# Variance products on the rounded squares and their remainder, placed one transpose later

## The chip, the cores and the metric

The kernel runs on one core of one Trainium2 chip. The metric is the device time of one execution in microseconds (us). The profile is one execution, recorded by the hardware profiler.

## The reference

The input is 8 sequences of 256 tokens with 128 channels. One attention layer of 16 heads comes first, then a stack of six layers, each with local attention (16 heads of 64, window 32) and a gated feed-forward part. The change lies in the feed-forward part's layer norm:

```python
def ffn_layer(x, g, bln, W1, b1, W2, b2):
    mu = x.mean(-1, keepdims=True)
    var = ((x - mu) ** 2).mean(-1, keepdims=True)
    xn = (x - mu) / jnp.sqrt(var + 1e-05) * g + bln
    hg = xn @ W1 + b1
    a, gate = jnp.split(hg, 2, -1)
    return a * jax.nn.gelu(gate, approximate=False) @ W2 + b2
for i in range(DEPTH):
    x = attn_layer(shift_tokens(x), Wqkv[i], q_scale[i], k_scale[i], Wo[i]) + x
    x = ffn_layer(shift_tokens(x), ln_g[i], ln_b[i], W1[i], b1[i], W2[i], b2[i]) + x
```

## The kernel before

After the first attention (some 280 us) the six layers are worked off as 6 x 8 = 48 units, one sequence in one layer each. A unit's activations lie as 128 channels (partitions) x 256 tokens, in two tiles `t` of 128 tokens. Every engine runs the same software pipeline: `step` works on four neighbouring units at once, `after`, `u` (projection, rope, transposes), `before` (softmax and values) and `last` (output projection, layer norm and feed-forward). The order inside `step` is written out by hand for each engine, and each engine works its own list strictly in that order. Semaphores (`signal`) tie the lists together: an engine that reaches a wait stops there, and so does all that stands behind it in its list.

The functions that matter, with the lines of the profile:

- TensorE, `proj(u, t, j)` (L1910, L1915, L1919): one of 16 projections of a unit into one of two PSUM banks. A bank is free again when the copy or rope that reads what lay in it is done: proj(u, 1, 1) waits for `un` on ScalarE, proj(u, 1, 2) and proj(u, 1, 3) wait for the two ropes of tile 1 on DVE.
- TensorE, `transpose_qk` (L1934): four transposes into the bank TP; waits for `normalise` on GpSimd and for the copy `qT` or `kT` on ScalarE that empties TP. `transpose_p` (L1966): eight transposes of the softmax.
- TensorE, `feed_mean` (L1999, L2000): x minus its mean, by a product with a centering matrix, into the bank FB. `feed_var` (L2009): the mean of the squares of each token, two products whose stationary operand is a tile of squares (128 x 128) and whose moving operand is one column of 1/128. `feed_turn` (L2018) transposes the reciprocal root back over all partitions. `feed_w1` (L2035 to L2037) is the first feed-forward product, on operands split into a rounded part and a remainder.
- ScalarE, `copy_center` (L1747, xc), `square_x` (L1754, xq), `copy_u` (L1660, un), `square` (L1650, sq), `copy_qkT` (L1672 qT, L1676 kT).
- DVE, `feed_3` (L1553): variance plus epsilon to `vtok`. Behind it in DVE's list stand `rope(u, 1, 0, 0)` and `rope(u, 1, 0, 1)` (L1486).
- GpSimd, `turn` (L1346, two halves), `normalise` (L1408), `feed_w1_lo` (L1399, in some of the units), `feed_rstd` (L1382, rtok = vtok to the power -0.5), `feed_lo` (L1389, xg_lo).

`F32R` is the format of the rounded operands, four bytes each; `F32` is full precision. The lists around the change, as they were before:

```python
# TensorE                      # GpSimd                 # DVE
transpose_qk(u, 0, 0, 0)       normalise(u, 0, 0)       soft_shift(before, 1)
feed_var(last)                 turn(u, 0, 1, 0)         feed_3(last)
proj(u, 1, 1)                  turn(u, 0, 1, 1)         rope(u, 1, 0, 0)
transpose_qk(u, 0, 0, 1)       feed_w1_lo(last)         rope(u, 1, 0, 1)
transpose_p(before, 0)         feed_rstd(last)          sums(u, 1, 0)
feed_turn(last)                normalise(u, 0, 1)       feed_norm(last)
```

Of the kernel before, what the change touches and what calls it, by code (L numbers as in the profile page):

```python
# [31 lines left out]
P = 128  # L32
# [57 lines left out]
def build(nc, x, w_heads, bq_heads, bk_heads, w_v, b_v_rows, w_proj, b_proj_rows, wqk, q_scale_rows, k_scale_rows, wvt, wo,  # L90
          feed_cols, w1, w2, rope, ident, win_mask, win_pick, causal, positions, slope_heads, one_row, weights, out):
    with ExitStack() as ctx:
        def sb(name, shape, dt=F32):
            return ctx.enter_context(nc.sbuf_tensor(name, shape, dt))

        def signal(name, per=1, start=0):
            return Signal(ctx.enter_context(nc.semaphore(name)), per, start)
# [89 lines left out]
        x2l_d = signal("x2l_d")  # L187
        xc_a = signal("xc_a")
        xq_a = signal("xq_a")
        var_p = signal("var_p")  # L190
        vr_d = signal("vr_d")
        rr_g = signal("rr_g")
# [1010 lines left out]
        xc = sb("xc", [P, T])  # L1203
        xe = sb("xe", [P, 2, T])
        xq = sb("xq", [P, T])
        vtok = sb("vtok", [P, TT])
        rtok = sb("rtok", [P, TT])
        xg = sb("xg", [P, T])
# [7 lines left out]
        def index(u):  # L1216

            return u[0] * 2 + u[1]
# [15 lines left out]
        def live(u):  # L1234

            n = index(u)
            return not isinstance(n, int) or 0 <= n < UNITS
# [7 lines left out]
        with nc.Block() as block:  # L1245
# [80 lines left out]
            def _(pool):  # L1326
# [50 lines left out]
                def feed_rstd(u):  # L1377
# [3 lines left out]
                    pool.wait_ge(vr_d.sem, vr_d.at(n))  # L1381
                    G.tensor_tensor(rtok[:, :], vtok[:, :], minus_half[:, :], ALU.pow).then_inc(rr_g.sem, 1)  # L1382

                def feed_lo(u):
                    if not live(u):
                        return
                    n = index(u)
                    pool.wait_ge(xgh_a.sem, xgh_a.at(n))
                    G.tensor_tensor(xg_lo[:, :], xg[:, :], xg_hi[:, :], ALU.subtract).then_inc(xgl_g.sem, 1)  # L1389
# [20 lines left out]
                def step(m, s):  # L1410
                    after, u, before, last = ((m, s + k) for k in (1, 0, -1, -2))
                    clamp(before, 1)
                    norms(before, 1, 0)
                    norms(before, 1, 1)
                    norms(before, 1, 2)
                    norms(before, 1, 3)
                    norms(before, 1, 4)
                    norms(before, 1, 5)
                    norms(before, 1, 6)
                    norms(before, 1, 7)  # L1420
                    normalise(before, 1, 0)
                    turn(before, 1, 1, 0)
                    turn(before, 1, 1, 1)
                    normalise(before, 1, 1)
                    turn(u, 0, 0, 0)
                    shift_lo(after)
                    turn(u, 0, 0, 1)
                    clamp(u, 0)
                    norms(u, 0, 0)
                    norms(u, 0, 1)  # L1430
                    norms(u, 0, 2)
                    norms(u, 0, 3)
                    norms(u, 0, 4)
                    norms(u, 0, 5)
                    norms(u, 0, 6)
                    norms(u, 0, 7)
                    normalise(u, 0, 0)
                    turn(u, 0, 1, 0)
                    turn(u, 0, 1, 1)
                    feed_w1_lo(last)  # L1440
                    feed_rstd(last)
                    normalise(u, 0, 1)
                    turn(u, 1, 0, 0)
                    turn(u, 1, 0, 1)
                    feed_lo(last)
# [4 lines left out]
            def _(dve):  # L1450
# [4 lines left out]
                dve.wait_ge(tables_ready.sem, 1)  # L1455
                dve.sem_inc(fin_d.sem, 1)
                dve.wait_ge(ident_in.sem, 16)
                V.tensor_scalar(center[:, :], ident_s[:, :], 1.0 / C, None, ALU.subtract).then_inc(center_d.sem, 1)

                def add_shifted(u, add):  # L1460
# [87 lines left out]
                def feed_3(u):  # L1548
                    if not live(u):
                        return  # L1550
                    n = index(u)
                    dve.wait_ge(var_p.sem, var_p.at(n))
                    V.tensor_scalar(vtok[:, :], ps[:, FB, T:T + TT], LN_EPS, None, ALU.add).then_inc(vr_d.sem, 1)  # L1553

                def feed_norm(u):
                    if not live(u):
# [79 lines left out]
            def _(act):  # L1636
# [112 lines left out]
                def square_x(u):  # L1749
                    if not live(u):  # L1750
                        return
                    n = index(u)
                    act.wait_ge(mean_p.sem, mean_p.at(n))
                    S.activation(xq[:, :], ps[:, FB, 0:T], ACT.Square).then_inc(xq_a.sem, 1)  # L1754

                def feed_scale(u):
# [103 lines left out]
            def _(pe):  # L1860
# [141 lines left out]
                def feed_var(u):  # L2002
                    if not live(u):
                        return
                    n = index(u)
                    pe.wait_ge(xc_a.sem, xc_a.at(n))
                    pe.wait_ge(xq_a.sem, xq_a.at(n))
                    for t in range(TT):
                        last = M.matmul(ps[:, FB, T + t:T + t + 1], xq[:, t * P:(t + 1) * P], mean_w[:, 0:1], start=True, stop=True)  # L2009
                    last.then_inc(var_p.sem, 1)  # L2010

                def feed_turn(u):
# [46 lines left out]
                def step(m, s):  # L2059
# [19 lines left out]
                    transpose_qk(u, 0, 0, 0)  # L2079
                    if index(last) == UNITS - 2:  # L2080
                        keep_warm(10, PJ)
                    feed_var(last)
                    if index(last) == UNITS - 1:
                        finish_turn(2)
                        finish_turn(3)
                    proj(u, 1, 1)
                    transpose_qk(u, 0, 0, 1)
                    transpose_p(before, 0)
                    feed_turn(last)
                    if index(last) == UNITS - 1:  # L2090
# [137 lines left out]
```

## Time and profile before

| | |
|---|---|
| median of 3 runs | 1670.52 us (1668.34 to 1673.65) |
| the profiled execution | 1671.68 us, span 1669.9 us |
| granted clock of TensorE, mean | 0.990 |
| TensorE matmul busy | 1621.9 us (97%) |
| TensorE weight load busy | 1412.5 us (85%) |
| DVE busy | 1478.7 us (89%) |
| ScalarE busy | 1327.9 us (80%) |
| GpSimd busy | 1333.4 us (80%) |

The span runs from the first to the last instruction; the time of an execution is a little longer. PE stands for TensorE's matmuls, PEld for its weight loads, which overlap them; ACT is ScalarE, POOL is GpSimd. In the timeline, bracketed text at a row's end is the idle time of that engine before it and what ended it. Matmul ends are modelled, so starts are the safer figures.

### The profile page before, as it was taken

The numbers are of one execution on the slowest core, as the hardware profiler recorded it, in microseconds if no ns is written. First come the engines' busy times: TensorE is split into PE (matmuls) and PEld (weight loads), VectorE is DVE, ScalarE is ACT, GpSimd is POOL, SyncE is SP. The second block draws the span as 40 slices with busy tenths as digits, with TensorE's granted clock in tenths as the row PEclk, the third lists the DMA queues.
The fourth block names the chain that finished last, engine by engine and source line by source line (L and its number), as shares of the span: only waits on it lengthen the run. The fifth ranks groups of instructions, "written<-read, shape, count | busy, mean of one in ns | idle before, by whom it ended". The sixth has DMA issues, their size and how long they took to land.

```text
span 1669.9 us, 70686 instructions
## 1 busy us (share of the span) xinstructions
PE 1621.9 (97%) x29222; PEld 1412.5 (85%) x29222; DVE 1478.7 (89%) x2314; ACT 1327.9 (80%) x2801; POOL 1333.4 (80%) x1810
## 2 busy tenths in 40 slices
PE   7999969999999999999999999999999999999997
PEld 5777647898989889898988889898898988889886
DVE  6887748999999999899999999999999999999984
ACT  6888836888878788887888788788888888888874
POOL 7777568888888888888888788888888888888870
PEclk9999979999999999999999999999999999999999
DMA  3588507566865656857566766658566567656654
GB/s 126 172 299 313 213 11 160 129 151 138 228 161 129 150 122 151 235 135 162 121 150 180 184 149 140 145 120 251 129 157 144 132 152 214 156 126 147 141 130 113
DMA packets 101407, 265.78 MB, mean 159 GB/s; under 512 B 26720, under 2 KB 34912, under 8 KB 101088
## 3 DMA queue, kind: packets, MB, share of 16 engines
q1 hardware_dynamic: 101088, 261.26, 61.9%
q8 instruction: 232, 3.80, 1.0%
q14 instruction: 87, 0.71, 0.1%
HBM read 45.15 MB, written 27.26 MB: 43 GB/s over the span
## 4 chain that ended last, share of the span: by engine, by line
PE 80%; POOL 2%; SPq 1%; issue 1%; DVE 1%; ACT 1%; DMA 0%; POOLq 0%; ACTq 0%; DVEq 0%
PE ps L1910 18%; PE ps L1919 14%; PE ps L1978 10%; PE ps L1934 10%; PE ps L1956 8%; PE ps L1966 5%; PE ps L2048 4%; PE ps L2035 2%; PE ps L2037 2%; PE ps L2036 2%; PE ps L1948 2%; SPq L1262 1%; PE ps L2009 1%; PE ps L1915 1%; PE ps L1989 1%
## 5 line engine op out<-in xcount | busy, mean ns | idle before, releaser
L1346 POOL TENSOR_TENSOR rot<-rot 128x512 f32<-128x512 f32 x380 | 491.4, 1309 | 43.5 <-DVE rot L1486 43.4
L1486 DVE TENSOR_TENSOR rot<-ps,rope_l 128x1024 f32<-128x1024 f32 x380 | 462.6, 1218 | 21.1 <-ACT sq L1650 13.0
L1408 POOL TENSOR_TENSOR rot<-rot,rnorm 128x1024 f32<-128x1024 f32 x190 | 361.9, 1905 | 17.7 <-POOL rnorm L1374 0.4
L1660 ACT ACTIVATE un<-ps 128x512 f32<-128x512 f32 x384 | 229.4, 597 | 105.4 <-PE ps L1910 42.3
L1910 PE MATMUL ps<-w_t,xs_hi 128*128 128x512 f32 x880 | 298.0, 419 | 3.7 <-DVE rot L1486 1.7
L1919 PE MATMUL ps<-w_t,xs_hi 128*128 128x256 f32 x1284 | 262.9, 297 | 14.2 <-PEq L375 11.0
L1650 ACT ACTIVATE sq<-ps 128x512 f32<-128x512 f32 x380 | 227.5, 599 | 48.8 <-PE ps L1910 27.4
L1472 DVE TENSOR_REDUCE ssum<-sq 128x16 f32<-128x1024 f32 x190 | 229.8, 1210 | 14.0 <-ACT sq L1650 14.0
L1934 PE MATMUL ps<-ident_s,rot 128*128 128x128 f32 x1536 | 233.9, 275 | 2.6 <-POOL rot L1408 1.1
L1919 PEld LDWEIGHTS ps<-w_t,xs_hi 128*128 128x128 f32 x1284 | 196.4, 190 | 24.6 <-issue 20.4
L1934 PEld LDWEIGHTS ps<-ident_s,rot 128*128 128x128 f32 x1536 | 179.3, 140 | 36.9 <-issue 17.3
L1978 PE MATMUL ps<-vk,pT 128*32 128x128 f32 (+1 forms) x6624 | 189.6, 267 | 0.6 <-ACT pT L1693 0.6
L1919 PE MATMUL ps<-w_t,xs_lo 128*128 128x256 f32 x642 | 180.6, 281 | 0.0
L1978 PEld LDWEIGHTS ps<-vk,pT 128*32 128x32 f32 x6624 | 163.9, 110 | 16.6 <-issue 15.6
L1910 PEld LDWEIGHTS ps<-w_t,xs_hi 128*128 128x128 f32 x880 | 139.1, 190 | 33.6 <-ACT un L1660 7.6
L1910 PE MATMUL ps<-w_t,xs_lo 128*128 128x512 f32 x389 | 154.5, 397 | 0.0
L1956 PEld LDWEIGHTS ps<-kT,qT 64*32 64x32 f32 x12288 | 146.8, 106 | 7.3 <-issue 1.2
L1956 PE MATMUL ps<-kT,qT 64*32 64x64 f32 x12288 | 149.7, 226 | 0.5 <-issue 0.5
L1919 PEld LDWEIGHTS ps<-w_t,xs_lo 128*128 128x128 f32 x642 | 121.4, 189 | 0.0
L1530 DVE TENSOR_TENSOR prob<-ps,linv 128x1024 f32<-128x1024 f32 x96 | 117.6, 1225 | 3.1
L1497 DVE TENSOR_REDUCE smax<-ps 128x16 f32<-128x1024 f32 x96 | 116.4, 1213 | 3.9 <-PE ps L1956 3.9
L1514 DVE TENSOR_REDUCE lsum<-ps 128x16 f32<-128x1024 f32 x96 | 116.6, 1215 | 2.7 <-ACT ps L1684 2.7
(158 smaller groups left out, 3572.0 us busy)
## 6 DMA issues: line engine op xcount, KB each, us to landing
vk<-un SPq DMA_DIRECT2D x1440, 128.0 KB
w_t<-weights_dram SPq DMA_DIRECT2D x48, 512.0 KB, 6.9
weights_dram<-rot SPq DMA_DIRECT2D x12, 1024.0 KB, 5.1
weights_dram<-sq SPq DMA_DIRECT2D x24, 512.0 KB, 3.5
raw<-wqk_dram SPq DMA_DIRECT2D x24, 256.0 KB, 4.2
wvt_s<-wvt_dram SPq DMA_DIRECT2D x12, 256.0 KB, 5.2
wo_s<-wo_dram SPq DMA_DIRECT2D x12, 256.0 KB, 6.4
w_s<-w_dram SPq DMA_DIRECT2D x6, 341.0 KB, 3.5
```

Source lines behind the costliest of these rows:

```text
L1346: last = G.tensor_tensor(cos[:, :, s, :], cos[:, :, s, :], sin[:, :, 1 - s, :], ALU.add)
L1408: G.tensor_tensor(v, v, rnorm[:, t, kind * H:(kind + 1) * H, None].broadcast_to([P, H, D]), ALU.mult).then_inc(nrm_g.sem, 1)
L1472: V.tensor_reduce(ssum[:, t, kind * H:(kind + 1) * H], sq[:, kind, :].rearrange("p (h e) -> p h e", h=H), AX_X, ALU.add).then_inc(ss_d.sem, 1)
L1486: V.tensor_tensor(dst, src[:, None, :, :].broadcast_to([P, 2, H // 2, D]), tab[:, :, None, :].broadcast_to([P, 2, H // 2, D]), ALU.mult).t ...
L1530: V.tensor_tensor(pairs, tile_scores(t).rearrange("p (hp a) k -> p hp a k", hp=2), inv, ALU.mult).then_inc(pn_d.sem, 1)
L1650: S.activation(sq[:, kind, half * 512:(half + 1) * 512], ps[:, PJ + PJ_BANK[t][2 * kind + half], :], ACT.Square).then_inc(sq_a.sem, 1)
L1660: S.activation(un[:, (u[1] % 2) * TT + t, j // 2, (j % 2) * HALF:(j % 2 + 1) * HALF], ps[:, PJ + PJ_BANK[t][QK_BANKS + j], :], ACT.Copy).t ...
L1910: last = M.matmul(bank, v, w_t[:, j, w, :], start=i == 0, stop=i == 2)
L1919: last = M.matmul(bank[:, cols], v, w_t[:, j, w, cols], start=i == 0, stop=i == 2)
L1934: last = M.transpose(ps[:, TP, a * P:(a + 1) * P], rot[:, kind, 0, c * P:(c + 1) * P], ident_s[:, :])
L1956: last = M.matmul(out_s, qT[rows, par, a, 32 * w:32 * w + 32], kT[rows, a, 32 * w:32 * w + 64], start=False, stop=a == PAIRS - 1)
L1978: last = M.matmul(ps[32 * k:32 * k + 32, SO[t], cols], pT[:, a, 32 * k:32 * k + 32], vk[:, 4 * t + k, a, cols], start=a == 0, stop=a == PA ...
```

## The change

The squares are written twice by ScalarE from the same PSUM bank, once rounded to F32R (`xq_hi`), once in full (`xq`). GpSimd subtracts the one from the other into `xq_lo`, F32R as well. Each variance product becomes two accumulating ones, with `xq_hi` and `xq_lo` as stationary operands, and the moving operand has two columns of 1/128 (`mean_r`), so that each result takes two columns of the bank, of which `feed_3` reads the first. `feed_var` waits for GpSimd's subtract in place of ScalarE's square, and stands two places later in TensorE's list. `square_lo` stands between the two halves of `turn(u, 0, 1)` on GpSimd.

```diff
+        xql_g = signal("xql_g")
...
+        xq_hi = sb("xq_hi", [P, T], F32R)
+        xq_lo = sb("xq_lo", [P, T], F32R)
+        mean_r = sb("mean_r", [P, 2], F32R)
...
+                def square_lo(u):
+                    if not live(u):
+                        return
+                    n = index(u)
+                    pool.wait_ge(xq_a.sem, xq_a.at(n))
+                    G.tensor_tensor(xq_lo[:, :], xq[:, :], xq_hi[:, :], ALU.subtract).then_inc(xql_g.sem, 1)
...
                     turn(u, 0, 1, 0)
+                    square_lo(last)
                     turn(u, 0, 1, 1)
...
+                V.tensor_copy(mean_r[:, :], mean_w[:, 0:2])
...
-                    V.tensor_scalar(vtok[:, :], ps[:, FB, T:T + TT], LN_EPS, None, ALU.add).then_inc(vr_d.sem, 1)
+                    V.tensor_scalar(vtok[:, :], ps[:, FB, T:T + 2 * TT].rearrange("p (t k) -> p t k", k=2)[:, :, 0], LN_EPS, None, ALU.add).then_inc(vr_d.sem, 1)
...
+                    S.activation(xq_hi[:, :], ps[:, FB, 0:T], ACT.Square)
                     S.activation(xq[:, :], ps[:, FB, 0:T], ACT.Square).then_inc(xq_a.sem, 1)
...
-                    pe.wait_ge(xq_a.sem, xq_a.at(n))
+                    pe.wait_ge(xql_g.sem, xql_g.at(n))
                     for t in range(TT):
-                        last = M.matmul(ps[:, FB, T + t:T + t + 1], xq[:, t * P:(t + 1) * P], mean_w[:, 0:1], start=True, stop=True)
+                        for i, v in enumerate((xq_hi, xq_lo)):
+                            last = M.matmul(ps[:, FB, T + 2 * t:T + 2 * t + 2], v[:, t * P:(t + 1) * P], mean_r[:, :], start=i == 0, stop=i == 1)
...
-                    feed_var(last)
...
                     proj(u, 1, 1)
                     transpose_qk(u, 0, 0, 1)
+                    feed_var(last)
                     transpose_p(before, 0)
                     feed_turn(last)
```

TensorE's list in a unit from the middle of the run, from the first transposes of the unit to feed_turn. The names in brackets are the semaphores waited for: `un_a1` is copy_u of tile 1, `qkT_a` the copy out of TP, `nrm_g` normalise, `pn_d` the softmax, `rr_g` rtok. Before:

```order
L1934 MATMUL ps<-ident_s,rot 128x128 [waits qkT_a,nrm_g]
L1934 MATMUL ps<-ident_s,rot 128x128 x3
L2009 MATMUL ps<-mean_w,xq 128x1 [waits xq_a,xc_a]
L2009 MATMUL ps<-mean_w,xq 128x1
L1910 MATMUL ps<-w_t,xs_hi 128x512 [waits un_a1]
L1910 MATMUL ps<-w_t,xs_hi 128x512
L1910 MATMUL ps<-w_t,xs_lo 128x512
L1934 MATMUL ps<-ident_s,rot 128x128 [waits qkT_a,nrm_g]
L1934 MATMUL ps<-ident_s,rot 128x128 x3
L1966 MATMUL ps<-ident_s,prob 128x128 [waits pn_d]
L1966 MATMUL ps<-ident_s,prob 128x128 x7
L2018 MATMUL ps<-ident_s,rtok 128x128 [waits rr_g]
```

With the change (the kernel's lines have other numbers there):

```order
L1924 MATMUL ps<-w_t,xs_hi 128x512 [waits un_a1]
L1924 MATMUL ps<-w_t,xs_hi 128x512
L1924 MATMUL ps<-w_t,xs_lo 128x512
L1948 MATMUL ps<-ident_s,rot 128x128 [waits qkT_a,nrm_g]
L1948 MATMUL ps<-ident_s,rot 128x128 x3
L2024 MATMUL ps<-mean_r,xq_hi 128x2 [waits xql_g,xc_a]
L2024 MATMUL ps<-mean_r,xq_lo 128x2
L2024 MATMUL ps<-mean_r,xq_hi 128x2
L2024 MATMUL ps<-mean_r,xq_lo 128x2
L1980 MATMUL ps<-ident_s,prob 128x128 [waits pn_d]
L1980 MATMUL ps<-ident_s,prob 128x128 x7
L2033 MATMUL ps<-ident_s,rtok 128x128 [waits rr_g]
```

The variance products left the place in front of proj(u, 1, 1) and stand behind the next four transposes, four single products in place of two, and they wait for `xql_g`.

GpSimd's list in the same place, in a unit with a piece of W1. Before:

```order
L1346 TENSOR_TENSOR rot<-rot 128x16x32 [waits rope_d]
L1346 TENSOR_TENSOR rot<-rot 128x16x32
L1399 TENSOR_TENSOR w_lo<-w_s,w_hi 128x226 [waits w1_p,w1h_a]
L1382 TENSOR_TENSOR rtok<-vtok,minus_half 128x2 [waits vr_d]
L1408 TENSOR_TENSOR rot<-rot,rnorm 128x1024 [waits newton_g,turn_g]
```

With the change:

```order
L1350 TENSOR_TENSOR rot<-rot 128x16x32 [waits rope_d]
L1393 TENSOR_TENSOR xq_lo<-xq,xq_hi 128x256 [waits xq_a]
L1350 TENSOR_TENSOR rot<-rot 128x16x32
L1410 TENSOR_TENSOR w_lo<-w_s,w_hi 128x226 [waits w1_p,w1h_a]
L1386 TENSOR_TENSOR rtok<-vtok,minus_half 128x2 [waits vr_d]
L1419 TENSOR_TENSOR rot<-rot,rnorm 128x1024 [waits newton_g,turn_g]
```

The subtract came between the two halves of the turn, with a wait of its own for ScalarE's squares (`xq_a`).

## Rows read from the trace of the kernel before

**Rows 1.** Windows view, one unit: us, busy PE, PEld, DVE, ACT, POOL; clock; DMA.

```profile
1256.05:1285.22 29.17, 29.17 (x570) 26.26 (x569) 27.37 (x32) 23.85 (x45) 24.28 (x33) 1.00 0.63 142
```

**Rows 2.** The chain that ended last: shares, then pieces (start us, us, what).

```profile
PE 80%; POOL 2%; SPq 1%; issue 1%; DVE 1%; ACT 1%; DMA 0%; POOLq 0%; ACTq 0%; DVEq 0%
...
1256.56 0.81 PE ps L1910 x3
...
1258.89 1.40 PE ps L1910 x6
```

**Rows 3.** Groups by line, and two rows of the timeline (start us, us).

```profile
L2009 PEld LDWEIGHTS ps<-mean_w,xq 128*128 128x128 f32 x192 | 25.2, 192 | 0.6 <-ACT xc L1747 0.6
L1999 PEld LDWEIGHTS ps<-x_hi,center 128*128 128x128 f32 x48 | 9.0, 188 | 3.4 <-DVE x_lo L1546 1.2 <-issue 0.4
...
1253.93 0.28 PE L1999 MATMUL ps<-x_hi,center 128*128 128x256 f32 x1
...
1254.05 0.28 PE L2000 MATMUL ps<-x_lo,center 128*128 128x256 f32 x1
```

**Rows 4.** The timeline, weight loads of TensorE: start us, us, engine, line, tiles.

```profile
1255.94 0.53 PEld L2009 LDWEIGHTS ps<-mean_w,xq 128*128 128x128 f32 x4
...
1256.39 0.30 PEld L1910 LDWEIGHTS ps<-w_t,xs_hi 128*128 128x128 f32 x2
...
1257.01 0.54 PEld L1934 LDWEIGHTS ps<-ident_s,rot 128*128 128x128 f32 x4
...
1257.53 0.91 PEld L1966 LDWEIGHTS ps<-ident_s,prob 128*128 128x128 f32 x8
...
1258.40 0.25 PEld L2018 LDWEIGHTS ps<-ident_s,rtok 128*128 128x128 f32 x2
...
1258.62 0.30 PEld L1910 LDWEIGHTS ps<-w_t,xs_hi 128*128 128x128 f32 x2
...
1259.31 0.30 PEld L1910 LDWEIGHTS ps<-w_t,xs_hi 128*128 128x128 f32 x2 [0.16 <-DVE rot L1486]
...
1259.89 0.59 PEld L1934 LDWEIGHTS ps<-ident_s,rot 128*128 128x128 f32 x4
...
1262.92 0.19 PEld L2035 LDWEIGHTS ps<-xg_hi,w_hi 128*128 128x128 f32 x1
```

**Rows 5.** The timeline, ScalarE.

```profile
1254.62 0.38 ACT L1747 ACTIVATE xc<-ps 128x256 f32<-128x256 f32 x1
...
1254.89 0.39 ACT L1754 ACTIVATE xq<-ps 128x256 f32<-128x256 f32 x1
...
1255.15 0.62 ACT L1660 ACTIVATE un<-ps 128x512 f32<-128x512 f32 x1
...
1255.81 0.60 ACT L1650 ACTIVATE sq<-ps 128x512 f32<-128x512 f32 x1
...
1256.31 0.59 ACT L1672 ACTIVATE qT<-ps 128x512 f32<-128x512 f32 x1
```

**Rows 6.** The timeline, DVE.

```profile
1256.59 0.16 DVE L1553 TENSOR_SCALAR vtok<-ps 128x2 f32<-128x2 f32 x1 [0.88 <-PE ps L2009]
1256.67 2.58 DVE L1486 TENSOR_TENSOR rot<-ps,rope_l 128x1024 f32<-128x1024 f32 x2
...
1262.09 2.43 DVE L1486 TENSOR_TENSOR rot<-ps,rope_l 128x1024 f32<-128x1024 f32 x2
```

**Rows 7.** The timeline, GpSimd.

```profile
1253.00 2.73 POOL L1346 TENSOR_TENSOR rot<-rot 128x512 f32<-128x512 f32 x2
...
1256.83 0.72 POOL L1382 TENSOR_TENSOR rtok<-vtok,minus_half 128x2 f32<-128x2 f32 x1 [1.11 <-DVE vtok L1553]
...
1257.52 1.90 POOL L1408 TENSOR_TENSOR rot<-rot,rnorm 128x1024 f32<-128x1024 f32 x1
...
1259.38 2.53 POOL L1346 TENSOR_TENSOR rot<-rot 128x512 f32<-128x512 f32 x2
...
1261.93 0.73 POOL L1389 TENSOR_TENSOR xg_lo<-xg,xg_hi 128x256 fp32r<-128x256 f32 x1
```

## Prediction

> **What bounds the kernel now.** I read the busy table of one steady unit first, then the chain that ended last, then the timeline of the stretch that the change touches, engine by engine.
>
> One unit of the pipeline (one sequence in one layer) takes 29.17 us [rows 1], from one variance product to the next, and 48 units make up most of the span. In it TensorE is busy all 29.17 us at a granted clock of 1.00, DVE 27.37, ScalarE 23.85, GpSimd 24.28. So TensorE has no slack, DVE has 1.80 us a unit, the other two about 5. The chain of the whole run agrees: 80% of it lies on TensorE [rows 2]. Hence two rules for costing: whatever makes TensorE wait, or adds passes to it, lengthens every unit; what another engine does longer costs nothing until its result comes later than TensorE asks for it. The averages don't say where that is, so the rest is a walk through the unit that starts at 1256.05.
>
> **The products themselves: 0 us.** The 96 variance products appear as 192 loads and 192 matmuls of one column [rows 3]: a full-precision product is already two passes here, so a unit has four. The products on tiles of the rounded format appear once each (center, x48 for 48 units), so four of them are four passes again. A load of 128 rounded columns takes 188 ns, of full ones 192 ns [rows 3]. The four loads hold the load queue for 1256.39 - 1255.94 = 0.45 us [rows 4]; products of the rounded format follow each other at 1254.05 - 1253.93 = 0.12 us [rows 3], so 0.48. I take 0.45 before and after.
>
> The Trainium skill, "TensorE: Matmul & The Clock Gate", section on weight-path perf modes, says that fast weight load is on for 128 weights of a type other than FP32 and measured about twice the speed. Taken for the rounded format, it would make the four loads about half as long, and an estimate by it is 0.22 us less for a unit. The 188 ns against 192 of rows 3 don't show it.
>
> **ScalarE squares twice: +0.27 us a unit, not hidden.** ScalarE's small operations overlap; they start 1254.89 - 1254.62 = 0.27 apart though each lasts 0.38 [rows 5]. So un, sq and qT behind the square start 0.27 later. un and sq run without a gap before them, and qT (the copy that frees the transpose bank) ends at 1256.90; the load of the next transposes starts at 1257.01, 0.11 later [rows 4, 5]. That load is therefore already held by ScalarE about as much as by TensorE's own order. With qT at 1256.58 + 0.59 = 1257.17 it starts at **1257.28 (+0.27)**. Taking the variance block away from in front of proj(1,1) brings nothing: TensorE is ready 0.45 earlier and then waits for this copy (proj(1,1) itself needs un, ready at 1256.04).
>
> **GpSimd's subtract: 0 us.** It waits for xq, which now ends at 1254.89 + 0.27 + 0.39 = 1255.55. A result reaches the next engine about 0.08 later, as vtok's end at 1256.75 does rtok's start at 1256.83 [rows 6, 7]. So it starts at 1255.63 and takes what xg_lo takes, 0.73 [rows 7]: ready at 1256.36. The products ask for it later than 1257.7. The second half of turn(0,1), half of the pair of 2.73, moves to 1256.36 to 1257.7. Behind it GpSimd stood idle 1.11 before rtok [rows 7] (less in units with a piece of w1_lo there), and rtok will wait longer still (below), so the 0.73 lies in that idle time. Without that cover it would cost 0.73 a unit.
>
> **The products move behind transpose_qk(0,0,1): this is the cost.** That transpose holds the load queue 1257.53 - 1257.01 = 0.52 [rows 4], so the variance loads start at 1257.28 + 0.52 = 1257.80 instead of 1255.94 (+1.86), and the transposes of transpose_p at 1258.25 instead of 1257.53 (+0.72). From the first variance load to vtok are 1256.59 - 1255.94 = 0.65 [rows 4, 6], so vtok starts at 1258.45. Two things hang on it.
>
> - DVE. Ahead of vtok in the queue DVE is idle, [0.88 <-PE ps L2009]; behind it stand the two ropes of tile 1 [rows 6], and they free the banks of proj(1,2) and proj(1,3). Now they start at 1258.45 + 0.08 = 1258.53. Without a wait between them two take 2.43 (the pair at 1262.09) [rows 6], so the first frees its bank at 1259.75, the second at 1260.96. Today the pair ends at 1256.67 + 2.58 = 1259.25 and the load of proj(1,3) starts at 1259.31 with [0.16 <-DVE rot L1486] [rows 4]: the bank is already the thing waited for. So it now starts at 1260.96 + 0.06 = 1261.02, **+1.71**. Proj(1,2) is held to 1259.81 (+1.19); its own 0.69 would let proj(1,3) start at 1260.50, so the second rope decides.
> - GpSimd. rtok starts at 1258.61 + 0.08 = 1258.69 and ends at 1259.41; feed_turn's load, 1258.40 today [rows 4], comes at 1259.50 (+1.10), which lies under the +1.19. normalise(0,1) starts 0.69 after rtok's start [rows 7] and ends at 1261.28; transpose_qk(0,1,0) asks for it at 1259.89 + 1.71 = 1261.60, so it doesn't wait. The next pair of turns starts 1.86 behind it, xg_lo 2.55 after that, at 1263.79, and ends at 1264.52; the load of the first W1 product asks at 1262.92 + 1.71 = 1264.63 [rows 4, 7]. Also just hidden.
>
> After that every engine is 1.7 to 1.8 behind, and none has anything to catch up with, TensorE having had no slack. The unit becomes 29.17 + 1.71 = 30.88 us.
>
> **Sum.** 46 units in which projections run beside it: 46 x 1.71 = 78.7. In the last two units none do; there the chain itself gets longer by 0.27 + 0.73 + 0.08 = 1.1, so 2.2. The copy of mean_w is one instruction. Total 81 us. The profiled execution took 1671.68 (span 1669.9): 1752.7. The median of the runs is 1.2 lower: **1752**, 4.9% slower. Below: if only one of the two late results counted, 1.10 a unit. Above: matmuls of the rounded format behind full ones start slowly, three take 0.81 there and 1.40 / 2 = 0.70 otherwise [rows 2]; the moved block makes one more such change, +0.11, and GpSimd's two hits with 0.1 to spare may miss by up to 0.3: 2.1 a unit. Forecast's own range 1.5 to 1.95 a unit: 1740 to 1761.
>
> **The rivals.**
> - *feed_turn alone decides* (0.12). The ropes' lateness is absorbed by DVE's 1.80 idle and TensorE waits just for rtok: 46 x 1.10 + 2.2 = 53, so 1723. For it: DVE's slack is about as large as its delay. Against: the slack lies before vtok, not behind it, and a wait on the rope is in the trace already.
> - *Not slower: TensorE alone decides, and loads of the rounded tiles pass in half the time* (0.06). The place is the block of four loads: 0.45 / 2 = 0.22 less, 48 times, 10.8 us: 1660; with full-length loads 1670.5, no change. It decides if a load takes under 0.1 us and the load of proj(1,3) isn't later than now. For it: averages leave every other engine room. Against: rows 3, and 0.88 of idle DVE in front of vtok can't pay for 1.86. The load rule of the Trainium skill's page named above points to this case; by it, with the waits as I walk them, the unit would grow by 1.49 instead of 1.71.
> - *More than forecast* (0.12): the slow start and GpSimd's misses come on top, 2.1 a unit: 1670.5 + 46 x 2.1 + 2.2 = 1769. The same price would follow if the edit didn't do what it says and a rounded product with two columns ran in two passes (0.45 more a unit); the x48 of center speaks against that.
>
> **How the numbers follow.** Forecast 0.70, the rivals 0.12, 0.06, 0.12. The range takes in most of both outer cases that are slower: 1720 to 1772. A change under 0.3% (5 us) can't be told from none with this kernel. Faster by more 0.03, within 0.03 (both from the second rival), slower 0.94.
>
> **What the changed profile would show.** Variance loads still x192, near 190 ns. DVE's idle time before vtok grows from 0.9 to about 2.7 us a unit, and TensorE's loads show waits for DVE's rot in front of proj(1,2) and proj(1,3), and a wait for ScalarE's qT in front of transpose_qk(0,0,1). GpSimd's waits for xq_a and vtok stay, without TensorE waiting for xq_lo. The unit is 30.9 us. I am wrong if proj(1,3) isn't waiting on rot, or if vtok starts less than 1.5 us later beside the transposes than it did.

## The result, and the profile after

The changed kernel takes 1736.72 us (median of 4 runs, 1734.71 to 1737.97), the kernel before 1671.64 in the same count of runs: ratio 1.0359, 95% interval 1.0329 to 1.0388. By the two medians it is 65 us slower; the ratio given is not the quotient of these two medians (1.0389, just above the interval) and stands for 60 us. 1752 was forecast, with a range of 1720 to 1772. The page of the changed kernel begins:

```profile
span 1732.9 us, 70783 instructions
...
PE 1665.7 (96%) x29222; PEld 1407.6 (81%) x29222; DVE 1473.0 (85%) x2315; ACT 1349.5 (78%) x2849; POOL 1365.6 (79%) x1858
```

The instruction counts of TensorE are those of before (29222), while the span grew by 63 us. Its busy time grew by 44 us of these for the same instructions, since the ends of its matmuls are modelled and hide part of a wait; the loads show the waits better. The windows view of one unit, in the columns of [rows 1]:

```profile
1297.69:1328.23 30.54, 30.18 (x572) 26.14 (x569) 27.29 (x32) 24.31 (x46) 24.96 (x35) 1.00 0.63 143
```

A unit now takes 30.5 us. Taken over all units, the distance from one vtok to the next has a median of 30.48 us against 29.16 before: **+1.32 a unit**, where 1.71 was forecast. The work of DVE and GpSimd in it is what it was plus the subtract. The loads of the variance products, in groups by line (they answer to [rows 3]):

```profile
L2024 PEld LDWEIGHTS ps<-mean_r,xq_lo 128*128 128x128 f32 x96 | 18.7, 195 | 0.0
L2024 PEld LDWEIGHTS ps<-mean_r,xq_hi 128*128 128x128 f32 x96 | 18.6, 194 | 1.1 <-issue 1.0
```

192 in all, at 194 to 195 ns: four passes a unit as before, and no shorter loads. The list of waits (who waited for whom, us in total, times, longest):

```profile
DVE vtok L1566 <- PE ps L2024: 114.1, 48, 2.8
POOL xq_lo L1393 <- ACT xq L1768: 76.7, 48, 16.8
...
PEld ps L1924 <- DVE rot L1499: 35.5, 83, 1.4
...
PEld ps L2033 <- POOL rtok L1386: 17.9, 48, 1.3
```

DVE's wait for the variance was 38.5 us before and is 114.1; TensorE's loads wait for ropes and for rtok. Now the same stretch as in [rows 4 to 7], from the timeline of the changed kernel (start us, us, engine, line). Its xc starts 40.14 later than in the unit of before, so 40.14 taken off brings both on one clock.

```profile
1294.76 0.38 ACT L1760 ACTIVATE xc<-ps 128x256 f32<-128x256 f32 x1
...
1295.29 0.41 ACT L1768 ACTIVATE xq<-ps 128x256 f32<-128x256 f32 x1
...
1295.77 0.73 POOL L1393 TENSOR_TENSOR xq_lo<-xq,xq_hi 128x256 fp32r<-128x256 f32 x1 [1.03 <-ACT xq L1768]
...
1296.50 0.65 ACT L1685 ACTIVATE qT<-ps 128x512 f32<-128x512 f32 x1
...
1297.27 0.42 PEld L1948 LDWEIGHTS ps<-ident_s,rot 128*128 128x128 f32 x4 [0.51 <-issue]
...
1297.66 0.19 PEld L2024 LDWEIGHTS ps<-mean_r,xq_hi 128*128 128x128 f32 x1
...
1298.13 0.86 PEld L1980 LDWEIGHTS ps<-ident_s,prob 128*128 128x128 f32 x8
...
1298.31 0.16 DVE L1566 TENSOR_SCALAR vtok<-ps 128x2 f32<-128x2 f32 x1 [2.33 <-PE ps L2024]
1298.39 2.36 DVE L1499 TENSOR_TENSOR rot<-ps,rope_l 128x1024 f32<-128x1024 f32 x2
1298.55 0.72 POOL L1386 TENSOR_TENSOR rtok<-vtok,minus_half 128x2 f32<-128x2 f32 x1 [0.81 <-DVE vtok L1566]
...
1299.32 0.19 PEld L2033 LDWEIGHTS ps<-ident_s,rtok 128*128 128x128 f32 x2 [0.33 <-POOL rtok L1386]
...
1299.67 0.30 PEld L1924 LDWEIGHTS ps<-w_t,xs_hi 128*128 128x128 f32 x2 [0.15 <-DVE rot L1499]
...
1300.80 0.30 PEld L1924 LDWEIGHTS ps<-w_t,xs_hi 128*128 128x128 f32 x2 [0.60 <-DVE rot L1499]
...
1301.38 0.59 PEld L1948 LDWEIGHTS ps<-ident_s,rot 128*128 128x128 f32 x4
...
1303.56 0.75 POOL L1400 TENSOR_TENSOR xg_lo<-xg,xg_hi 128x256 fp32r<-128x256 f32 x1
...
1304.41 0.19 PEld L2050 LDWEIGHTS ps<-xg_hi,w_hi 128*128 128x128 f32 x1
```

| on the clock of before | before | forecast | measured |
|---|---|---|---|
| qT ends | 1256.90 | 1257.17 | 1257.01 |
| load of transpose_qk(0,0,1) | 1257.01 | 1257.28 | 1257.13 |
| first variance load | 1255.94 | 1257.80 | 1257.52 |
| load of transpose_p | 1257.53 | 1258.25 | 1257.99 |
| vtok starts | 1256.59 | 1258.45 | 1258.17 |
| second rope ends | 1259.25 | 1260.96 | 1260.61 |
| load of feed_turn | 1258.40 | 1259.50 | 1259.18 |
| load of proj(1,3) | 1259.31 | 1261.02 | 1260.66 |
| load of transpose_qk(0,1,0) | 1259.89 | 1261.60 | 1261.24 |
| xg_lo starts | 1261.93 | 1263.79 | 1263.42 |
| first W1 load | 1262.92 | 1264.63 | 1264.27 |

The order of events is the forecast one to the last row; the loss is 1.35 where 1.71 stood. The load of proj(1,3) carries the wait named, [0.60 <-DVE rot L1499]. In front of transpose_qk(0,0,1) the row says "issue" (0.51) and names nobody; that this is the wait for qT is read from qT's end, 0.12 before that load.

The pipeline's last unit does something that the walk hadn't seen:

```profile
1714.47 0.57 PE L2071 MATMUL ps<-ident_s,xe 128*128 128x128 f32 x2 [0.43 <-ACT xe L1809]
1714.70 0.35 PE L2024 MATMUL ps<-mean_r,xq_hi 128*128 128x2 f32 x1
```

The products stand behind finish_turn(2) and finish_turn(3) now (L2071), which the edit moved them past, and these wait for ScalarE's copies. The last two distances between vtoks grew by 0.88 and 3.95 us (27.36 and 23.35, before 26.48 and 19.40), not by 2.2 together. That place is not all of it. e2 below has it too, and its last two distances are 26.28 and 21.08. The same 64 products of `values`, behind the vtok of the last unit but one, in the change and in e2:

```profile
1694.41 3.47 PE L1992 MATMUL ps<-vk,pT 128*32 128x128 f32 x64 [0.59 <-ACT pT L1706]
```

```profile
1687.36 1.95 PE L1978 MATMUL ps<-vk,pT 128*32 128x128 f32 x64 [0.57 <-ACT pT L1693]
```

The granted clock of the stretch around them was 0.70 in the change (1692.38 to 1698.00) and 1.00 in e2 (1685.35 to 1691.00), which is 1.5 us of the 3.95. What brought the clock down there is open.

### The profile page after: what moved, and what is told of

Read it like the earlier page. It is cut to its first block, busy times and chain, and to the rows that moved or that the text cites. A ratio compares the mean times of both kernels' runs of the same rounds, so it can differ in the third digit from the quotient of the medians.

```text
span 1732.9 us, 70783 instructions
## 1 busy us (share of the span) xinstructions
PE 1665.7 (96%) x29222; PEld 1407.6 (81%) x29222; DVE 1473.0 (85%) x2315; ACT 1349.5 (78%) x2849; POOL 1365.6 (79%) x1858
## 4 chain that ended last, share of the span: by engine, by line
PE 76%; issue 4%; DVE 4%; POOL 1%; ACT 1%; POOLq 0%; ACTq 0%; DVEq 0%
PE ps L1924 17%; PE ps L1933 13%; PE ps L1992 10%; PE ps L1948 10%; PE ps L1970 7%; PE ps L2063 4%; DVE rot L1499 4%; PE ps L1980 2%; PE ps L2050 2%; PE ps L2052 2%; PE ps L2051 2%; PE ps L1962 2%; PE ps L2024 1%; PE ps L1929 1%; PE ps L2003 1%
## 5 line engine op out<-in xcount | busy, mean ns | idle before, releaser
L1499 DVE TENSOR_TENSOR rot<-ps,rope_l 128x1024 f32<-128x1024 f32 x380 | 458.3, 1217 | 11.6 <-ACT sq L1663 9.3
L1419 POOL TENSOR_TENSOR rot<-rot,rnorm 128x1024 f32<-128x1024 f32 x190 | 361.8, 1904 | 17.4
L1924 PE MATMUL ps<-w_t,xs_hi 128*128 128x512 f32 x880 | 305.0, 427 | 9.3 <-DVE rot L1499 9.3
L1706 ACT ACTIVATE pT<-ps 128x1024 f32<-128x1024 f32 x96 | 98.5, 1026 | 35.9 <-PE ps L1980 35.9
L1685 ACT ACTIVATE qT<-ps 128x512 f32<-128x512 f32 x192 | 116.9, 609 | 6.9 <-PE ps L1948 0.5
```

Source lines behind the costliest of these rows:

```text
L1419: G.tensor_tensor(v, v, rnorm[:, t, kind * H:(kind + 1) * H, None].broadcast_to([P, H, D]), ALU.mult).then_inc(nrm_g.sem, 1)
L1499: V.tensor_tensor(dst, src[:, None, :, :].broadcast_to([P, 2, H // 2, D]), tab[:, :, None, :].broadcast_to([P, 2, H // 2, D]), ALU.mult).t ...
L1924: last = M.matmul(bank, v, w_t[:, j, w, :], start=i == 0, stop=i == 2)
```

## The experiments

Each was timed beside the kernel before on its own chip. The last column is the median distance from one vtok to the next.

| run | time, us | ratio to before, 95% | a unit, us |
|---|---|---|---|
| the change | 1736.7 | 1.0359 [1.0329, 1.0388] | 30.48 |
| e1_place_back | 1704.8 | 1.0175 [1.0148, 1.0203] | 29.73 |
| e2_move_only | 1726.9 | 1.0303 [1.0280, 1.0327] | 30.40 |
| e3_square_only | 1680.5 | 1.0027 [1.0012, 1.0043] | 29.18 |
| e4_vtok_between_ropes | 1735.0 | 1.0352 [1.0328, 1.0375] | 30.50 |
| e5_two_products | 1700.7 | 1.0142 [1.0117, 1.0167] | 29.03 |
| e7_gpsimd_branch_freed | 1742.6 | 1.0389 [1.0367, 1.0411] | 30.64 |
| e8_both_branches_freed | 1711.9 | 1.0208 [1.0184, 1.0232] | 29.87 |
| e9_variance_broadcast | 3722.2 | 2.2199 [2.2135, 2.2263] | |
| e10_subtract_unread | 1701.3 | 1.0180 [1.0150, 1.0209] | 29.71 |
| e11_four_rounded | 1675.0 | 1.0006 [0.9986, 1.0025] | 29.15 |
| e12_two_products_shifted | 1703.1 | 1.0180 [1.0157, 1.0203] | 29.05 |
| e13_in_the_gap | 1711.3 | 1.0221 [1.0195, 1.0247] | 29.84 |

### Place and split, one at a time

e1, on the changed kernel:

```diff
+                    feed_var(last)
                     proj(u, 1, 1)
                     transpose_qk(u, 0, 0, 1)
-                    feed_var(last)
```

> The changed kernel with the variance products back in front of proj(u,1,1); squares, subtract and rounded products stay. Theory (the late place holds the two ropes on DVE, and with them proj(1,2) and proj(1,3)): the place costs most of the 1.32 us a unit. Back in front, TensorE waits for xq_lo instead: ready at 1256.38 in the unit's clock of before, asked for at 1255.94, so about +0.5 a unit, 24 us, 1695, and vtok starts at 1257.1. Rival (the split itself, squares and subtract, costs the time wherever the products stand): stays near 1737.

e2, on the kernel before:

```diff
-                    feed_var(last)
                     proj(u, 1, 1)
                     transpose_qk(u, 0, 0, 1)
+                    feed_var(last)
```

> The kernel before with its full-precision variance products moved behind transpose_qk(u,0,0,1), nothing else. Theory: the move alone brings the loss, less the 0.13 to 0.14 a unit by which the second square holds qT: +1.2 a unit, 57 us, about 1729, DVE idle before vtok more than 2 us a unit. Rival (the split costs it): 1672 to 1680.

e3, on the kernel before:

```diff
+        xq_hi = sb("xq_hi", [P, T], F32R)
...
+                    S.activation(xq_hi[:, :], ps[:, FB, 0:T], ACT.Square)
                     S.activation(xq[:, :], ps[:, FB, 0:T], ACT.Square).then_inc(xq_a.sem, 1)
```

> The kernel before with a second square on ScalarE that nobody reads; nothing else. Theory: un, sq and qT come 0.1 to 0.2 later and hold the load of transpose_qk(0,0,1), +0.14 a unit, 6.7 us, 1678. Rival (ScalarE's slack hides it): 1671.6. Upper bound by the start distance of 0.27 a unit: 1685.

e2 came out as the theory had it: the move alone, without any split, makes a unit 1.24 us longer (30.40) and brings the whole picture. Three rows of its timeline:

```profile
1292.89 0.42 PEld L1934 LDWEIGHTS ps<-ident_s,rot 128*128 128x128 f32 x4 [0.54 <-issue]
...
1293.93 0.16 DVE L1553 TENSOR_SCALAR vtok<-ps 128x2 f32<-128x2 f32 x1 [2.35 <-PE ps L2009]
...
1296.42 0.30 PEld L1910 LDWEIGHTS ps<-w_t,xs_hi 128*128 128x128 f32 x2 [0.60 <-DVE rot L1486]
```

The transposes start after 0.54 of idle load queue even without the second square, vtok comes after 2.35 us of idle DVE (before: 0.88), and proj(1,3) waits for the rope. What the split adds at the late place is 30.48 - 30.40 = 0.08 in the median unit. Over the whole run it is more, 9.7 us between the two profiled spans (1732.9 and 1723.2; the ratios, 1.0359 and 1.0303, give 9.4): some 5 in the units, whose means differ by 0.11, and 3.4 in the last two.

e3 lies between: 1.0027, its interval clear of 1, but its median unit is 29.18 against 29.16. So the second square doesn't hold every unit by 0.14, which was expected; most of the 4.5 us is in a few single units of 31.5 to 32.7 us (before has one of 31.3), in which a load of TensorE starts late with nobody waited for. More on these below.

e1 gave back more than half: +0.57 a unit, where 0.5 was expected. Two things are late in its timeline:

```profile
1277.64 1.27 POOL L1350 TENSOR_TENSOR rot<-rot 128x512 f32<-128x512 f32 x1
...
1277.80 0.19 PEld L2024 LDWEIGHTS ps<-mean_r,xq_hi 128*128 128x128 f32 x1 [0.51 <-issue]
...
1278.87 0.72 POOL L1386 TENSOR_TENSOR rtok<-vtok,minus_half 128x2 f32<-128x2 f32 x1
```

TensorE's load of the products starts after 0.51 us of idle queue, waiting for xq_lo, as expected. But GpSimd has no idle time left in front of rtok, where before it had 1.11 [rows 7]. So either could be the cost.

### Whose queue pays at the old place

e10, on the kernel before: second square and subtract are there, nobody reads them, the products are the full-precision ones and wait for the squares alone.

```diff
...
+                    S.activation(xq_hi[:, :], ps[:, FB, 0:T], ACT.Square)
                     S.activation(xq[:, :], ps[:, FB, 0:T], ACT.Square).then_inc(xq_a.sem, 1)
...
                     turn(u, 0, 1, 0)
+                    square_lo(last)
                     turn(u, 0, 1, 1)
```

> The kernel before with the second square and GpSimd's subtract, both unread: the products stay full precision at their old place and wait for the squares alone. The run with the place put back lost 0.6 us a unit; two causes are possible. Theory A (GpSimd's queue: the subtract and its wait push the second half of the turn, rtok, normalise and xg_lo back by 0.4 to 0.7): +0.4 to 0.6 a unit here too, 1690 to 1700. Theory B (only TensorE's wait for xq_lo at the products counts): as with the second square alone, 1672 to 1680.

Theory A: 29.71, the same as with the place put back (29.73). TensorE's wait for xq_lo, which only e1 has, costs nothing beyond it. The timeline of e10:

```profile
1216.36 0.73 POOL L1392 TENSOR_TENSOR xq_lo<-xq,xq_hi 128x256 fp32r<-128x256 f32 x1 [1.02 <-ACT xq L1766]
...
1217.05 1.29 POOL L1349 TENSOR_TENSOR rot<-rot 128x512 f32<-128x512 f32 x1
...
1218.29 0.73 POOL L1385 TENSOR_TENSOR rtok<-vtok,minus_half 128x2 f32<-128x2 f32 x1
...
1220.94 0.42 PEld L1946 LDWEIGHTS ps<-ident_s,rot 128*128 128x128 f32 x4 [0.35 <-POOL rot L1418]
...
1224.12 0.19 PEld L2047 LDWEIGHTS ps<-xg_hi,w_hi 128*128 128x128 f32 x1 [0.29 <-POOL xg_lo L1399]
```

The subtract waits for the squares and takes the rest of the idle time; from there GpSimd runs without a gap through turn, rtok and normalise, and TensorE waits for it twice, 0.35 at transpose_qk(0,1,0) and 0.29 at the first W1 product. So a subtract of 0.73 us put down to "0, hidden" costs 0.53 a unit where the variance is early (29.71 against 29.18 with the second square alone, e3). It is not its 0.73 alone: the second half of the turn stands behind its wait too, 1.02 + 0.73 = 1.75 us, and GpSimd's idle time in front of rtok was 1.11 [rows 7], which leaves 0.64 uncovered. In the change it is nearly free only because the late vtok costs more.

### The late vtok has two branches

e4, on the changed kernel:

```diff
-                    feed_3(last)
...
                     rope(u, 1, 0, 0)
+                    feed_3(last)
                     rope(u, 1, 0, 1)
```

> The changed kernel with feed_3 (vtok) between the two ropes of tile 1 in DVE's list instead of in front of both. Theory: the first rope no longer waits for the variance, the second starts at 1299.6 less 1.2 as before, so proj(1,3) is 0.24 late by it; now rtok holds feed_turn, 0.80 late: +0.8 a unit, 38 us, 1710. Rival (rtok and feed_turn set the time anyway, the ropes are only noted as waits): stays at 1737. Rival (TensorE's own added 0.5 in front of transpose_p is all that counts): 1695.

Nothing was gained (30.50), against the 0.5 a unit expected. The prediction's main wait is gone all the same, as the timeline shows:

```profile
1299.19 0.16 DVE L1566 TENSOR_SCALAR vtok<-ps 128x2 f32<-128x2 f32 x1 [0.38 <-PE ps L2024]
...
1300.93 0.42 PEld L1924 LDWEIGHTS ps<-w_t,xs_hi 128*128 128x128 f32 x2
...
1302.07 0.42 PEld L1948 LDWEIGHTS ps<-ident_s,rot 128*128 128x128 f32 x4 [0.49 <-POOL rot L1419]
...
1305.25 0.19 PEld L2050 LDWEIGHTS ps<-xg_hi,w_hi 128*128 128x128 f32 x1 [0.29 <-POOL xg_lo L1400]
```

The load of proj(1,3) at 1300.93 has no wait. In its place TensorE waits 0.49 for normalise (L1419) and 0.29 for xg_lo: GpSimd's list behind rtok. The first rival of this run got the number right, but feed_turn is not where it ends: its load waits as it did in the change (17.9 us in all in both), and rtok's lateness is passed on from there through normalise and xg_lo. In the change these two come in time by 0.25 us (normalise ends at 1301.13, asked for at 1301.38) and 0.10 (xg_lo ends at 1304.31, asked for at 1304.41), so GpSimd's branch is hardly shorter than the ropes'.

e7 frees this branch and leaves the ropes; e8 frees both, on the changed kernel:

```diff
# GpSimd, both
                     turn(u, 0, 1, 1)
+                    normalise(u, 0, 1)
                     feed_w1_lo(last)
                     feed_rstd(last)
-                    normalise(u, 0, 1)
# TensorE, both
-                    feed_turn(last)
...
                     proj(u, 1, 2)
                     proj(u, 1, 3)
+                    feed_turn(last)
# DVE, e8 alone: feed_3 between the two ropes, as in e4
```

> The changed kernel with normalise(0,1) in front of rtok in GpSimd's list and feed_turn behind proj(1,3) in TensorE's; the ropes still stand behind vtok. Theory after the last run (the late vtok acts through two branches of about equal length, ropes to proj(1,3), and rtok, normalise, turn, xg_lo to transpose_qk(0,1,0) and the first W1 product): freeing one alone gives nothing, 1733 to 1738. Rival (GpSimd's branch was the only one): about +0.5 a unit, 1695.

> As the run before, and vtok between the two ropes on DVE. Two-branch theory: both are gone, what stays is TensorE's own 0.5 a unit in front of transpose_p (the qT wait with nothing to fill it), and up to 0.2 where xg_lo is late: 1695 to 1705. Rival (a third path, feed_turn to xg on DVE and ScalarE, or the ropes' other readers, is as long): stays above 1725.

e7: nothing gained (30.64, if anything 0.16 more), with both projections held by ropes:

```profile
1306.23 0.30 PEld L1924 LDWEIGHTS ps<-w_t,xs_hi 128*128 128x128 f32 x2 [0.68 <-DVE rot L1499]
...
1307.36 0.30 PEld L1924 LDWEIGHTS ps<-w_t,xs_hi 128*128 128x128 f32 x2 [0.60 <-DVE rot L1499]
```

e8: 29.87, 25 us faster than the change. Neither branch alone, both together: each was long enough to hold the unit by itself. 1711.9 is above the 1705 expected, in part because the kernel before took 1677.6 beside it; by the ratio it is 1706 on the chip of the change. Its loads:

```profile
1287.86 0.30 PEld L1924 LDWEIGHTS ps<-w_t,xs_hi 128*128 128x128 f32 x2 [0.18 <-DVE rot L1499]
...
1288.64 0.19 PEld L2033 LDWEIGHTS ps<-ident_s,rtok 128*128 128x128 f32 x2 [0.25 <-POOL rtok L1386]
```

The ropes hold 0.18, as they did before the change (0.16 [rows 4]); rtok, now behind normalise, holds feed_turn 0.25. e13, on e8, asks whether the rest is TensorE's idle time in front of transpose_qk(0,0,1):

```diff
                     proj(u, 1, 1)
+                    feed_var(last)
                     transpose_qk(u, 0, 0, 1)
-                    feed_var(last)
```

> The run with both branches freed, and the products one place earlier, between proj(1,1) and transpose_qk(0,0,1), where TensorE stood 0.5 us a unit waiting for ScalarE's qT; the whole split stays. If the 0.7 a unit left in the run with both branches freed is that hole, which the four passes (0.45) now fill, the unit falls from 29.87 to 29.3 or 29.4, about 1680 to 1685. If it is GpSimd's longer list (rtok to feed_turn, xg_lo) or the split itself, it stays at 29.7 or more, 1700.

It isn't: 29.84. Rows of TensorE's loads and of GpSimd:

```profile
1284.72 0.42 PEld L1948 LDWEIGHTS ps<-ident_s,rot 128*128 128x128 f32 x4
...
1287.79 0.19 PEld L2033 LDWEIGHTS ps<-ident_s,rtok 128*128 128x128 f32 x2 [0.49 <-POOL rtok L1386]
```

```profile
1283.10 0.73 POOL L1393 TENSOR_TENSOR xq_lo<-xq,xq_hi 128x256 fp32r<-128x256 f32 x1 [1.06 <-ACT xq L1768]
...
1287.01 0.72 POOL L1386 TENSOR_TENSOR rtok<-vtok,minus_half 128x2 f32<-128x2 f32 x1
```

That idle time is filled (no wait at 1284.72) and the time comes back as 0.49 of waiting for rtok. The subtract stands between the two halves of the turn, sits idle 1.06 there until the squares come, and all behind it is late by that. These waits point to GpSimd's list for what is left in e8 and e13, as in e10; it isn't shown by a run, since a subtract behind the second half of the turn wasn't tried.

### What the products cost

e5, on the kernel before: the squares are rounded and the remainder is left out.

```diff
-        xq = sb("xq", [P, T])
+        xq = sb("xq", [P, T], F32R)
+        mean_r = sb("mean_r", [P, 2], F32R)
...
-                        last = M.matmul(ps[:, FB, T + t:T + t + 1], xq[:, t * P:(t + 1) * P], mean_w[:, 0:1], start=True, stop=True)
+                        last = M.matmul(ps[:, FB, T + 2 * t:T + 2 * t + 2], xq[:, t * P:(t + 1) * P], mean_r[:, :], start=True, stop=True)
```

> The kernel before, products at their old place, but the squares are rounded once and the remainder is left out (so the variance is that of rounded squares): two rounded products a unit in place of two full ones, 96 passes instead of 192, no second square, no subtract. If every pass of TensorE counts, 0.22 us a unit less: 10.8 us, 1661 to 1665. If the load of transpose_qk(0,0,1) is held by ScalarE's qT anyway, most of it is given back there: -0.1 a unit or less, 0 to -5 us.

e11 issues each of these two products twice, e12 has 16 more transposes ahead of the first unit (keep_warm of 26 in place of 10):

> The run with two rounded products, each issued twice: four passes a unit on rounded weights again, at the old place, one square, no subtract (the remainder is left out). Shows what four rounded passes cost against four passes of full products. Prediction's reading (no difference): median unit 29.16, time 1670 to 1680. And the long units of the two-product run, in which TensorE stood at an issue wait of 1 to 4.5 us: if they come from the faster pace of its units (28.87), they are gone here; if they come from the edit itself, they stay, and it is 1700.

> The run with two rounded products, with 16 more idle transposes ahead of the first unit, which move all later instructions of TensorE by 32 places and cost about 2 us once. If the long units hang on where the instructions lie, their number and places change and the time moves by more than 5 us from 1700; if they hang on the pace, it stays at about 1700 plus 2.

e11 equals the kernel before (1.0006, unit 29.15): four rounded passes cost what two full products cost, as the prediction had it. e5 missed both expectations. Its undisturbed units are shorter, 28.85 to 28.9, but the median is 29.03 and the time 1.4% longer, since in many units TensorE simply stops. The longest stop and the group in the list of waits:

```profile
924.13 0.14 PEld L1958 LDWEIGHTS ps<-kT,qT 64*32 64x32 f32 x3 [4.45 <-issue]
```

```profile
PEld ps L1958 <- issue: 19.8, 19, 4.4
```

Nobody is waited for there ("issue"); most of the stops fall into runs of short matmuls with a load each. Before has none on that line above 0.6 us. e12 moved all instructions by 32 places. Its median is 1703.1 against 1700.7, its ratio 1.0180 against 1.0142, and e5's own runs lie between 1694 and 1708, so the time tells little. The total on that line stayed:

```profile
PEld ps L1958 <- issue: 19.6, 9, 5.8
```

But the places of the stops tell more. One of e12:

```profile
926.09 0.25 PEld L1958 LDWEIGHTS ps<-kT,qT 64*32 64x32 f32 x19 [2.78 <-issue]
```

In e5 three pairs of load and matmul of that run were still to come at 924.13, in e12 nineteen: sixteen more, as many as were put in ahead. Counted from the start of the program it is the same place, behind 14977 matmuls in both. Two more places agree in this way, behind 12452 matmuls (at 786.8 us in both) and behind 19517 (1165.7 and 1172.2). The other stops of over 1 us in e5 are whole multiples of about 252 records of TensorE (loads and matmuls) apart, within 5. e11 and the kernel before have one behind the same 10504th matmul (3.26 and 1.14 us of idle load queue), e11 and e3 behind the 15044th. So a stop hangs on its place in TensorE's list: e12 moved the work by 32 places, and these three stayed at the same counts. The page counts 232 packets of the queue named "instruction", 16.4 KB each; TensorE's 58444 records (x29222 twice) make 252 for each of them, if that queue is TensorE's. By this estimate the stops lie where TensorE's list passes from one packet of instructions to the next. That they are waits for the next packet fits, but no run shows it, and why they are so many more with two passes fewer is open.

e9, on the kernel before:

```diff
...
-                    for t in range(TT):
-                        last = M.matmul(ps[:, FB, T + t:T + t + 1], xq[:, t * P:(t + 1) * P], mean_w[:, 0:1], start=True, stop=True)
+                    last = M.matmul(ps[:, FB, T:2 * T], mean_w[:, :], xq[:, :], start=True, stop=True)
...
-                    G.tensor_tensor(rtok[:, :], vtok[:, :], minus_half[:, :], ALU.pow).then_inc(rr_g.sem, 1)
+                    G.tensor_tensor(rtok[:, :], vtok[:, :], minus_half[:, 0:1].broadcast_to([P, T]), ALU.pow).then_inc(rr_g.sem, 1)
...
-                    feed_turn(last)
```

> A way to spend fewer passes, on the kernel before: the mean weights (128x128, all 1/128) are the stationary operand and the squares (256 columns, full precision) move, so the variance comes out on all partitions and feed_turn falls away; DVE adds epsilon to 256 columns, GpSimd takes the power of 256 columns instead of 2. TensorE: two passes and 0.43 us instead of 0.45 + 0.22, -0.2 a unit, 10 us, if GpSimd's power stays under about 1.5 us (its subtract of 256 columns takes 0.73, its power of 2 columns 0.72): 1662. Rival (the power takes several us for 256 columns and holds normalise and the rest): slower by that, 1700 to 1900.

The rival, far beyond its range. GpSimd's power of 256 columns, by line:

```profile
L1382 POOL TENSOR_TENSOR rtok<-vtok,minus_half 128x256 f32<-128x256 f32 x48 | 1975.2, 41150 | 93.6 <-DVE vtok L1553 93.6
```

41.15 us each, 0.16 us a column, where its subtract of the same size takes 0.73. (The exponent is one column read for all 256 there; no other form was run.) 48 of them make 1975 of the 2045 us lost; the granted clock was 0.73 on average, TensorE being idle half of the time.

e9 also shows what a full product costs when its moving operand is wide, at a granted clock of 1.00:

```profile
1299.46 0.60 PE L2008 MATMUL ps<-xq,mean_w 128*128 128x256 f32 x2
```

One of its two passes lasts 0.38 us by the trace, so they start 0.60 - 0.38 = 0.22 apart; rounded ones of 256 columns start 0.12 apart [rows 3]. The projection behind it agrees: its third matmul starts at 1300.37, 0.91 after this product, where first and third are otherwise 0.47 apart. A full product of 256 columns thus takes about 0.44, two rounded ones 0.24. That four rounded passes cost what two full products do holds for the one or two moving columns here.

## Why the prediction was right, and where it was off

- **Bound.** "Whatever makes TensorE wait lengthens every unit" held in every run but the two with fewer passes, where the stops outweigh what the clean units gain.
- **Products, 0 us.** Right: x192 loads of 194 to 195 ns, and e11. No faster load shows. By the Trainium skill, "TensorE: Matmul & The Clock Gate", section on weight-path perf modes, fast weight load is on for 128 weights of a type other than FP32 and measured about twice as fast. The same section says that it reads 32 bits at a time, with no win for FP32. The 194 to 195 ns agree with the second sentence for the rounded format, whose elements have four bytes too, and disagree with the first if that format counts as other than FP32.
- **ScalarE, +0.27.** Mis-sized. The start distance of 0.27 was right (1294.76, 1295.02 and 1295.29 for the three), and un came 0.26 late. But sq then followed un by 0.48 where it had been 0.66 before, so two thirds of it were caught up: something other than un had held sq, and the reading "without a gap" was wrong. The load of the transposes came 0.12 late, and e3 shows 0.02 in the median unit.
- **Subtract, 0 us.** Right for the change to within 0.08 in the median unit (e2 against the change), wrong as a general price: e10 has 0.53 beyond the second square. The sentence "without that cover it would cost 0.73" names the right dependence, but leaves out the wait for the squares, which stood in the forecast's own walk: the subtract at 1255.63, GpSimd free from about 1254.4.
- **The late place.** Right in mechanism, 0.36 too dear. The transposes hold the load queue 1297.66 - 1297.27 = 0.39 and not 0.52: after a wait the four loads are recorded as 0.42 (0.51 and 0.20 of idle queue ahead of them in the change, 0.54 in e2), right behind projections as 0.54 to 0.59. In e13 they take 0.42 behind the short variance products without a wait, so it is the work ahead of them that matters. Two ropes took 2.36 and not 2.43. With the 0.15 from ScalarE that is 0.13 + 0.07 + 0.15 = 0.35 of the 0.36.
- **GpSimd "just hidden".** The numbers held (no wait at transpose_qk(0,1,0) or W1 in the change). "0.1 to spare" for both is not what the walk gives, 0.32 and 0.11; measured are 0.25 and 0.10. The reading "the second rope decides" was half of it: e4 and e7 show two branches of nearly equal length.
- **The ends.** 2.2 us forecast, 4.8 measured, and by other causes. In the last unit the products stand behind two finish turns, a queue position that the walk left out: with the same position e2 takes 3.11 from xc to vtok where the kernel before takes 1.41, and the change 3.82. Another 1.5 goes with the granted clock of 0.70 behind the vtok before. In the last unit but one the products start after 0.83 of waiting for xq_lo, the wait said to stay away; the distance grew by 0.88.
- **Sum.** 45 distances at 1.30 on average are 58.4, the ends 4.8: 63.2, against 63.0 in the two profiled spans (1732.9 - 1669.9). The forecast's "1740 to 1761" for 1.5 to 1.95 a unit leaves out its own 2.2 for the ends: 1742 to 1762.
- **The rivals.** The first (1723, feed_turn alone) fell: the ropes hold both projections in the change, and e7, in which rtok no longer holds TensorE's list ahead of them, gains nothing. The second fell with e2 and e11. Of the third nothing was seen: no wait of GpSimd's came on top, and a slower start of the rounded format behind full ones can't be told from the table.

No version here beats the kernel before; e11 equals it.

## What to carry to other kernels

When a product is moved later, follow its result through every queue that has something standing behind it, and price all branches: if two come out nearly alike (here within 0.1 us), freeing one gains nothing, and only a run that frees both shows what the move costs. An operation hidden in another engine's idle time is hidden only as long as what ends that idle time stays late; cost it once with the cover and once without. When the operation also waits for something, what stands behind it pays for that wait as well. Count the passes in the trace, and how far apart they start, before splitting an operand to save some: with one moving column a full product was two passes and two rounded products cost just as much, with 256 columns a full pass took nearly twice as long as a rounded one.

## What was not expected

- TensorE stops of 1 to 5.8 us with nothing waited for, in the runs with two passes fewer a unit (e5, e12): clean units 0.3 us shorter, the whole 1.4 to 1.8% longer. They sit at fixed places of TensorE's list, whole multiples of about 252 records apart. A kernel at 100% of its bound isn't sure to gain from less work.
- GpSimd's power costs 0.16 us a column (41.15 us for 256), while 2 columns take 0.72.
